# Second mixture of a four-layer gated cross-attention kernel: replicates behind the routers, two slots ahead of the routing, one key tensor per pass

## The reference

```python
x = x + tanh(g_xattn[2]) * _L2_xattn_ref(_layernorm(x), ctx, ctx, mask, ...)   # 16 heads of 8
x = x + tanh(g_ffn[2])   * _L2_ffn_ref(_layernorm(x), gate_w, w13_weight, w2_weight)
x = x + tanh(g_xattn[3]) * _L3_xattn_ref(_layernorm(x), ctx, ...)              # 16 heads of 8
```

```python
scores = softmax(x @ gate_w.T, axis=-1)                  # 8 experts, 4 groups of 2
topk_ids, topk_w = _grouped_topk(scores)                 # best 2 groups, best 2 experts
combine = zeros((T, 8)).at[arange(T)[:, None], topk_ids].add(topk_w)
gu = einsum('th,eih->tei', x, w13_weight)                # 2 x 256 per expert
gate, up = gu[..., :256], gu[..., 256:]
act = silu(gate) * up * combine[:, :, None]
out = einsum('tei,ehi->th', act, w2_weight)
```

## Time and profile before

| | us |
|---|---|
| median of three timed runs | 467.68 |
| lowest and highest of them | 460.12, 469.45 |
| the profiled execution | 459.39 |
| its span, first to last instruction | 457.6 |
| busy: PE, DVE, ACT, POOL | 417.9, 329.8, 215.4, 142.7 |
| mean granted TensorE clock | 0.978 |

### The profile page before, as it was taken

How to read it: one execution, slowest core, us unless ns; L and a number is a source line. 1 busy time by engine, 2 the same in 40 slices (tenths; PEclk the granted TensorE clock), 3 DMA queues, 4 the chain that set the end, 5 groups by cost and what they waited for, 6 DMA issues and landing times.

```text
span 457.6 us, 6370 instructions
## 1 busy us (share of the span) xinstructions
PE 417.9 (91%) x2197; PEld 306.6 (67%) x2214; DVE 329.8 (72%) x695; ACT 215.4 (47%) x385; POOL 142.7 (31%) x126
## 2 busy tenths in 40 slices
PE   7988859886999999999999997799999988999986
PEld 3666628654777777754798984566666644799845
DVE  5556891876566666677766469799999997777376
ACT  2204222276788888751744412244444322655354
POOL 4100282130344344221100037156566534000062
PEclk9999988998999999999999987999999999999999
DMA  6600000001110011100010000011110000000001
GB/s 203 256 1 1 0 1 26 22 1 52 46 46 27 25 43 37 34 1 1 0 36 1 1 1 1 3 37 35 41 63 0 1 1 0 1 0 1 2 0 46
DMA packets 8639, 12.54 MB, mean 27 GB/s; under 512 B 1131, under 2 KB 4757, under 8 KB 8613
## 3 DMA queue, kind: packets, MB, share of 16 engines
q1 hardware_dynamic: 7984, 11.58, 7.7%
q10 hardware_dynamic: 533, 0.31, 0.2%
q0 software_dynamic: 96, 0.32, 0.2%
HBM read 11.54 MB, written 0.52 MB: 26 GB/s over the span
## 4 chain that ended last, share of the span: by engine, by line
PE 55%; DVE 28%; issue 7%; ACT 4%; POOL 4%; DMA 1%; ACTq 0%; DVEq 0%; POOLq 0%
PE bank L1605 7%; PE bank L1224 5%; PE bank L1225 5%; PE bank L1226 5%; PE bank L1495 4%; PE bank L1492 3%; PE bank L1231 3%; PE bank L1587 3%; PE bank L1496 3%; DVE shared L1170 3%; DVE rhi L1173 2%; DVE h L818 2%; DVE wa L1061 2%; POOL rstd L365 2%; DVE stats L806 2%
## 5 line engine op out<-in xcount | busy, mean ns | idle before, releaser
L1087 DVE TENSOR_TENSOR rlo<-bank,rhi 128x512 fp32r<-128x512 f32 x64 | 44.0, 690 | 37.0 <-ACT rhi L661 36.3
L365 POOL TENSOR_TENSOR rstd<-var,neghalf 128x4 f32<-128x4 f32 x16 | 16.2, 1014 | 156.8 <-DVE var L811 156.8
L1231 PE MATMUL bank<-heat 128*128 128x512 bf16 x209 | 58.5, 402 | 3.1 <-DVE heat L841 1.5
L1224 PE MATMUL bank<-hhi,wuh 128*128 128x512 f32 x128 | 51.6, 403 | 5.9 <-issue 3.3
L438 POOL TENSOR_TENSOR wb<-wb,wa 128x512 f32<-128x512 f32 x28 | 37.1, 1324 | 57.9 <-DVE wa L1061 57.9
L1225 PE MATMUL bank<-hlo,wuh 128*128 128x512 f32 x128 | 50.8, 397 | 0.0
L1226 PE MATMUL bank<-hhi,wul 128*128 128x512 f32 x128 | 50.6, 395 | 0.0
L675 ACT ACTIVATE bank<-bank,b1s 128x512 f32<-128x512 f32 x64 | 42.4, 663 | 8.2 <-PE bank L1226 7.3
L1492 PE MATMUL bank<-rhi,wdh 128*128 128x512 f32 x96 | 39.9, 416 | 2.6 <-DVE rlo L1176 1.2
L1495 PE MATMUL bank<-rlo,wdh 128*128 128x512 f32 x96 | 41.0, 427 | 0.0
L1140 DVE TENSOR_REDUCE small<-bank 128x6 f32<-128x462 f32 (+1 forms) x48 | 27.7, 578 | 18.1 <-PE bank L1226 18.1
(11 more groups left out here) (280 smaller groups left out, 887.1 us busy)
## 6 DMA issues: line engine op xcount, KB each, us to landing
up_raw<-in_w SPq DMA_DIRECT2D x8, 258.0 KB, 2.7
down_raw<-in_w SPq DMA_DIRECT2D x8, 256.0 KB, 2.8
up_raw<-in_v SPq DMA_DIRECT2D x8, 256.0 KB, 2.7
down_raw<-in_v SPq DMA_DIRECT2D x8, 128.0 KB, 2.8
const<-in_const SPq DMA_DIRECT2D x1, 913.0 KB, 6.9
mats<-in_mats SPq DMA_DIRECT2D x1, 640.0 KB, 5.2
mats<-in_mats SPq DMA_DIRECT2D x1, 576.0 KB, 4.0
x<-in_x SPq DMA_DIRECT2D x2, 256.0 KB, 3.4
```

What stands on the lines that cost most here:

```text
L1087: V.tensor_tensor(rlo[n % 4][:, :], bank[BANKS1[n % 4]][:, :], rhi[n % 4][:, :].bitcast(F32), ALU.subtract).then_inc(q["lo"], 1)
L1224: mm(o, lh, rh, start=start, stop=False)
L1231: mm(o[:, :], heat[:, 0:P], heat[:, :], start=True, stop=True)
```

## The change

Four things are rearranged; what is computed stays.

- The two `replicate` steps move behind the routers on TensorE, into banks 0 and 4, and ACT copies their result behind the two copies of `hT`. The heaters at these places change from 3, 2 and 10 to 8 and 6.
- VectorE runs slots 0 and 1 before `route2`. TensorE's `weights_T` moves from slots 0 and 1 to 2 and 3, ACT's copy and transfer from slots 2 and 3 to 4 and 5. TensorE forms the hidden products of slots 0 and 1 without heaters between them and has six behind.
- The three key tensors leave GpSimd's head: each pass has one, at slot 4.
- GpSimd's loop over passes 1 and 2 is written out.

```diff
--- before.py
+++ after.py
@@ -287,7 +287,7 @@
         BANKG, BANKU = [1, 2], [3, 7]
         BANKC = [5, 6]
 
-        BANKV = {(0, 0): 5, (0, 1): 2, (1, 0): 7, (1, 1): 3}
+        BANKV = {(0, 0): 5, (0, 1): 2, (1, 0): 0, (1, 1): 4}
 
 
         @block.sync
@@ -468,8 +468,6 @@
                 nc.gpsimd.memset(acc[b][:, :], 0.0).then_inc(m["zero"], 1)
             pool.wait_ge(kv["hi"], 2)
             pool.wait_ge(at["S"], 3 * NT * B)
-            for b, part in ((0, 0), (0, 1), (1, 0)):
-                key(b, part)
             mask_values(1, 0)
             pool.wait_ge(m["zero"], B)
 
@@ -487,13 +485,11 @@
                         low(n, r["hi"], N2 * i + n + 1, r["loP"])
                     if n % 2 == 1:
                         add(i, (n - 1) // 2 - 2, G2, r["mult"], r["add"])
-                    if i_is(i, 0) and n == 4:
-                        key(1, 1)
-
-            body2(0, False)
-            with pool.Fori(1, PASSES - 1) as i:
-                body2(i, False)
-            body2(PASSES - 1, True)
+                    if n == 4:
+                        key(i // 2, i % 2)
+
+            for i in range(PASSES):
+                body2(i, i == PASSES - 1)
             for k in range(12, 14):
                 norm(k)
             mask_values(1, 1)
@@ -729,16 +725,16 @@
 
             attend(0)
             for b in range(B):
+                transposed(10 + b)
+            for b in range(B):
                 replicated(1, b)
-            for b in range(B):
-                transposed(10 + b)
             exponentials(1)
 
             def body2(i, last):
                 for n, (p, b, c) in enumerate(CH2):
                     g = N2 * i + n
-                    if i_is(i, 0) and n in (2, 3):
-                        weights_T(1, n - 2)
+                    if i_is(i, 0) and n in (4, 5):
+                        weights_T(1, n - 4)
                     if n == 0:
                         up_hi(i, 1, 1, N2, r, r["g"])
                     if n == 2:
@@ -1161,7 +1157,6 @@
             for b in range(B):
                 parts(10 + b, b)
             logits(1)
-            route2()
 
             def body2(i, last):
                 for n in range(N2):
@@ -1177,6 +1172,8 @@
                                         ALU.subtract).then_inc(r["loD"], 1)
                     if n % 2 == 1:
                         weigh(i, (n - 1) // 2 - 2, G2, r["ys"], r["row"], r["mult"])
+                    if i_is(i, 0) and n == 1:
+                        route2()
 
             body2(0, False)
             with dve.Fori(1, PASSES - 1) as i:
@@ -1649,15 +1646,14 @@
                 output_of(1)
 
             attend(0)
+            pe.wait_ge(kv["act"], 2)
+            for b in range(B):
+                keep_busy(bank[6], (8, 6)[b])
+                transposes(10 + b)
+            for b in range(B):
+                router(1, b, 10 + b)
             for b in range(B):
                 replicate(1, b)
-            for b in range(B):
-                keep_busy(bank[6], (3, 2)[b])
-                transposes(10 + b)
-            pe.wait_ge(kv["reps"], 4)
-            for b in range(B):
-                router(1, b, 10 + b)
-            keep_busy(bank[6], 10)
 
             def hidden2(i, n):
 
@@ -1677,8 +1673,8 @@
                         hidden2(i, n + LAG2)
                     elif not last:
                         hidden2(i + 1, n + LAG2 - N2)
-                    if i_is(i, 0) and n in (0, 1):
-                        weights_T(1, n)
+                    if i_is(i, 0) and n in (2, 3):
+                        weights_T(1, n - 2)
                     if n in LO_POOL2:
                         down(i, n, last, C2, G2, r, r["loP"], len(LO_POOL2) * i + before(LO_POOL2, n + 1))
                     else:
@@ -1688,7 +1684,8 @@
             pe.wait_ge(m["split"], 2 * B)
             for n in range(LAG2):
                 hidden2(0, n)
-                keep_busy(bank[4], 10 * (1 - n))
+            pe.wait_ge(kv["reps"], 4)
+            keep_busy(bank[4], 6)
             body2(0, False)
             with pe.Fori(1, PASSES - 1) as i:
                 body2(i, False)
```

## The result

| | before | after |
|---|---|---|
| median of timed runs, us | 465.75 (4 runs, 460.12 to 469.45) | 480.73 (4 runs, 473.92 to 486.65) |
| profiled execution, us | 459.39 | 477.93 |
| its span, us | 457.6 | 476.1 |
| busy: PE, DVE, ACT, POOL | 417.9, 329.8, 215.4, 142.7 | 428.3, 327.6, 215.7, 141.6 |
| mean granted clock | 0.978 | 0.950 |

The ratio of the times is 1.0319, with a 95 % interval of 1.0204 to 1.0433. The forecast was 479.0 us and slower by over 2 %.

What follows compares the result with a forecast made beforehand. VectorE was taken to bound the middle passes, a chain of waits the head before them. Terms 2.8 + 3.9 + 4.8 = 11.5 us, put on the median 467.68, gave 479.2, taken as 479; range 465 to 485.

Steps and rivals of the forecast that it cites:

- `parts` undisturbed: Second mixture's head, VectorE: without key tensors there, `hhi` and `hlo` take 0.43 and 0.69, ending at 275.7 instead of 282.0.
- Replicates on the path: Head, TensorE: replicates behind the routers, mostly at half clock, delay the first hidden product to 283.1, 1.0 us later than before.
- T: Start of slot 2 in pass 0, after two slots and the routing: forecast at 299.5, against 296.74 before.
- H: Stretch from the attention's last output products to the multiply of slot 2 in pass 0: forecast plus 2.8 us.
- The combine weights: Pass 0: transposes, copies and transfers of `cflat` two slots later make `down` of slot 3 wait: plus 3.9 us.
- M: Stretch from the multiply of slot 2 to that of slot 6: forecast 13.6 us against 9.74, plus 3.9.
- The keys: Passes 1 to 3: one key tensor each delays VectorE by 1.34, 1.34 and 2.1 us, plus 4.8 in all.
- P: Stretch from the multiply of slot 6 to the mixture's last add on VectorE: forecast plus 4.8 us.
- The base: Median of three timed runs of the kernel before, 467.68 us, onto which the forecast put 11.5.
- The clock did not hold: Rival, chance 0.20: TensorE's clock holds through routers and replicates in the head; plus 6.5 us, 474.2.
- The keys were not free: Rival, chance 0.08: key tensors cost nothing in the passes; plus 6.7 us, 474.4.
- VectorE's own work did not decide: Rival, chance 0.12: VectorE's own work decides throughout, slot 0 waiting for VectorE alone; minus 2.7 us, 465.0.

Runs made afterwards that it cites:

- e1: The changed kernel with its three spread key tensors put back at GpSimd's head, the fourth staying in pass 0: 477.68 us, ratio 1.0246 to before.
- e2: The changed kernel with the replicates back ahead of the transposes on TensorE and their copies ahead of those of `hT`: median 475.55 us, no ratio.
- e6: The kernel before with only the replicates moved behind the routers, with their banks, copies and heaters: 466.50 us, ratio 1.0103 to before.
- e3: The changed kernel with the routing back ahead of slot 0 and `weights_T` back in slots 0 and 1: 474.48 us, ratio 1.0142 to before.
- e7: The kernel before with only slots 0 and 1 ahead of the routing and `weights_T` in slots 2 and 3: 476.33 us, ratio 1.0274 to before.
- e4: The changed kernel with 24 heater matmuls ahead of the hidden product of slot 4, during the routing: 478.92 us, ratio 1.0233 to before.
- e5: The kernel before with only the key tensors moved, one in each pass and none at GpSimd's head: 463.83 us, ratio 1.0039 to before.
- e8: The kernel before with one key tensor per pass and replicates, then eight heaters, behind the hidden products of slots 0 and 1: 467.29 us, ratio 1.0102 to before.
- e9: e8 without the eight heaters behind the replicates: 464.66 us, ratio 1.0097 to before.
- e10: e9 with the first key tensor made ahead of the mixture and none in pass 3: 464.32 us, ratio 1.0029 to before.
- e11: e10 with each batch's replicates behind one hidden product, and five heaters behind them: 466.42 us, ratio 0.9900 to before.

## Why the prediction was right, and where it was not

**`parts` undisturbed: right.** 0.42 and 0.69, at an end of 9.7 us behind the cut; I had put it at 10.0 (275.7).

**Replicates on the path: right, with two errors, of 0.9 and 0.8, that cancel by luck.** I had the first hidden product 17.4 us behind the cut (283.1), it started at 18.26. The clock fell where I let it, 8.35 behind the cut (8.5 forecast), inside the routers; two quarter microseconds of the kernel after, and the row ahead of them with TensorE's idle time:

```profile
278.50:278.75 0.25, 0.25 (x4) 0.25 (x3) 0.25 (x1) 0.00 (x0) 0.00 (x0) 1.00 0.00 0
278.75:279.00 0.25, 0.25 (x3) 0.25 (x3) 0.25 (x2) 0.00 (x0) 0.00 (x0) 0.50 0.00 0
...
276.96 0.90 PE L1234 MATMUL bank<-const,h 128*128 128x128 f32 x4 [1.88 <-DVE h L814]
```

TensorE is busy throughout these two, but it had stood idle for 1.88 us until 1.8 us before the fall; whether that idle time or the routers brought it about, no run separates.

The 16 router pieces took 2.42 in the chain where I had 2.3, a replicate piece 0.21 (8.56 / 40) where I took 0.20, 0.6 for the forty, and the routers began 0.15 later. From there to the first multiply 3.58 us (forecast 3.55). The routing then took 9.2 us, from 295.13 to 304.31, where I allowed 9.6: the split `rlo` of 295.30 stretched `ex` to 1.05, the small `wdl` stretched `gt` to 0.47 and no more. T fell 15.6 behind that product instead of 16.4: about half of that is the routing, the rest slots 0 and 1, for which 16.4 left 6.8 and which took 6.5. H came out at +2.82 against +2.8; e1, e2 and e6 show that the replicates carry it.

**The combine weights: the mechanism right, the size wrong.** M grew by 6.34, not 3.9, and e3 and e7 confirm that this is the order of the weights. Two steps failed: "I take 2.05 us to landing", which was 0.8 too short, and, larger, the 1.4, 1.4 and 0.65 us that I gave to `down` of slot 3, the hidden product of slot 6 and its silu, at full clock, 1.7 too short. The issue of the second transfer came 8.1 us behind T, inside my 7.2 to 9.3. From there to the landing it took 2.83. I had the bytes' movement from the earlier trace rows and "a little for the signal"; here the quarter microseconds of the kernel after show that this was the wrong half to look at:

```profile
313.50:313.75 0.25, 0.00 (x0) 0.00 (x0) 0.25 (x1) 0.10 (x1) 0.25 (x1) 1.00 0.17 66
313.75:314.00 0.25, 0.00 (x0) 0.00 (x0) 0.25 (x1) 0.00 (x0) 0.25 (x1) 1.00 0.18 66
314.00:314.25 0.25, 0.00 (x0) 0.00 (x0) 0.25 (x1) 0.00 (x0) 0.25 (x1) 1.00 0.00 0
```

The bytes moved between 313.5 and 314.0, 1.2 to 1.7 us behind the issue, and TensorE was released at 315.14, more than 1.1 us behind the last byte. That is 0.8 of the missing 2.4. The rest lies behind the landing: I let the clock recover once, early or late, in the products ahead of the transfer. It did (0.40 from 309.46), but TensorE then waited 3.52 us, and at 316.3 the clock fell a second time. From the second piece of `down` of slot 3 to the end of the hidden product of slot 6 the pieces took 0.61 to 0.63, and from the landing to the multiply of slot 6 it took 5.2 us, where I had 3.45. The row product between the pieces of `down` (0.43 in the chain) was not a term of its own. e4 removes the first low stretch only and gets 1.27 us.

**The keys: right.** P +4.67 against +4.8. Pass 1 grew by 1.86 and pass 2 by 1.41, where I had 1.34 each; pass 3 by 1.67, where I had 2.1 (its `rlo` waited 1.94, and a little of that was slack). e1 and e5 confirm 5.1 and 4.9.

**The base: lucky.** The forecast put 11.5 us onto the median of three runs, 467.68. With one more run that median is 465.75, and the measured ratio makes 14.9 us of it, near the 13.8 that H + M + P show. So 479.0 is near 480.73 because a base 1.9 too high met a sum 2.3 to 3.4 too low.

**The rivals.** The clock did not hold (0.60 from 276 to 290). (That rival's own sum is 0.4 off: 279.3 + 6.1 + 9.6 is 295.0, not 295.4.) The keys were not free, in the passes. VectorE's own work did not decide: it idled 11.44 us. In e8 TensorE had no idle time of note from its first hidden product at 284.87 to the fall of the clock at 293.5, just behind the 40 replicate pieces. The Trainium skill, "TensorE: Matmul & The Clock Gate", section "Why this matters for your kernels", has the rule that idle gaps between bursts cost the clock. Beside that row of e8 it is not the whole of it; for the fall in the kernel after, with 1.88 us idle ahead of it, it can't be ruled out. What property of the small products makes the clock fall was not tried. What the profiles show, one for each kernel, is that it fell inside a block of 40 that began at full clock or within 0.5 us of the block's end, in all seven kernels that have one (before, e2, e5, e7, e8, e9, e10), and not beside the two halves in e11.

## What to carry to other kernels

Work that runs on another engine is free only where the engine that it disturbs has slack, or does operations that the disturbance doesn't reach: the same key tensor cost 0 ahead of the mixture and 1.4 to 1.9 us in its passes. Filling a wait of the bounding engine (2.25 us here) by moving its work ahead delays what the moved-over step feeds; follow that result through every copy, transfer and wait to its first user before counting the gain. It can pay to put runs of tiny products between wide ones and not in one block: here it gave 2.86 us, in one pair of profiles (e10, e11).

## What the runs showed of the hardware

- A matmul piece with 24 columns and its own weights takes 0.11 us at 2.4 GHz (4.54 / 40) and 0.21 to 0.22 at 1.2 GHz (8.56 and 8.71 / 40). I had expected less than a doubling.
- A block of 40 such pieces was followed by the low clock even behind twelve wide fp32 pieces and with no idle time ahead of it (e8: eight heaters in 3.17 us at 293.03; e9: 0.77 and 0.63 at 290.31, there behind 1.29 us of idle time).
- A transfer of 32 KB from SBUF to SBUF took 2.83 us from issue to release, more than 1.1 of it behind the last byte; in e1, e2, e4 and e7, which wait for it too, it took 2.80 to 2.83.
- The program ahead of the cut, which is the same from the kernel before to e9, took 265.73 to 274.36 us; the kernel before, at the lower end, also has the highest mean clock (0.978, 0.932 to 0.967 in the others).
